# A graph network's messages scattered as two float32r parts in place of one f32 product

## The reference, cut to what matters

```python
# x (3125, 128), src and dst (53125,) with dst sorted, edge_vector (53125, 64)
for k in range(3):
    e = edge_vector @ edge_W[k] + edge_b[k]
    msg = relu(x[src] + e)
    agg = segment_sum(msg, dst, num_segments=n)
    z = (1.0 + eps[k]) * x + agg
    h = relu(batch_norm(z @ W1[k] + b1[k]))
    x = relu(layer_norm(h @ W2[k] + b2[k]))
result = layernorm(x_first + x)
```

## Time and profile before

| | |
|---|---|
| median of three timed runs | 2043.3 us |
| span of the profiled execution, first to last instruction | 1647.0 us |
| mean granted TensorE clock in it | 1.000 |
| PE / PEld busy | 1342.2 / 1215.3 us |
| POOL busy | 1182.0 us |
| DVE busy | 513.6 us |
| ACT busy | 312.8 us |

### The profile page before, as it was taken

The page is one execution under the profiler, slowest core; times in us unless marked ns, Lnnn a source line. Parts: engine busy times, 40 slices in busy tenths (PEclk is TensorE's granted clock), DMA queues, the critical chain, the costliest instruction groups (busy, mean ns, idle before and its releaser), DMA issues.

```text
span 1647.0 us, 21498 instructions
## 1 busy us (share of the span) xinstructions
PE 1342.2 (81%) x5618; PEld 1215.3 (74%) x5619; DVE 513.6 (31%) x1374; ACT 312.8 (19%) x638; POOL 1182.0 (72%) x1256
## 2 busy tenths in 40 slices
PE   0999988888887688888888888768888888888871
PEld 0999877777776677777777777657777777777761
DVE  3333323332233123333322333312333332232226
ACT  1121211211211112112211122111211211221111
POOL 7777777777775577777777777647777777777770
DMA  7343333333332233333333333323323223323332
GB/s 136 78 95 83 81 81 81 82 88 85 85 81 72 54 80 81 81 81 81 81 81 81 81 82 84 77 59 78 78 78 78 78 78 78 78 78 78 78 78 54
DMA packets 72207, 132.16 MB, mean 80 GB/s; under 512 B 33684, under 2 KB 47104, under 8 KB 67072
## 3 DMA queue, kind: packets, MB, share of 16 engines
q0 software_dynamic: 39936, 81.87, 18.6%
q10 hardware_dynamic: 17065, 46.37, 11.7%
q1 hardware_dynamic: 15191, 3.75, 1.4%
HBM read 127.06 MB, written 4.83 MB: 80 GB/s over the span
## 4 chain that ended last, share of the span: by engine, by line
POOL 65%; issue 24%; PE 4%; DMA 3%; DVE 2%; POOLq 1%; ACT 1%; ACTq 0%; DVEq 0%
POOL rows L255 65%; DMA x_in<-x_dram 2%; PE ps L664 2%; PE ps L689 1%; POOLq L206 1%; DVE wide L643 0%; DMA rows<-table_dram,src_t 0%; DVE stats L633 0%; PE ps L712 0%; POOLq L207 0%; PE ps L698 0%; PE ps L705 0%; DVE x_in L631 0%; POOLq L283 0%; DMA rows<-x_dram,src_t 0%
## 5 line engine op out<-in xcount | busy, mean ns | idle before, releaser
L255 POOL DMA_INDIRECT rows<-table_dram,src_t x832 | 785.8, 945 | 292.8 <-issue 292.8
L689 PE MATMUL ps<-onehot,msg 128*128 128x64 f32 x2496 | 600.9, 422 | 174.2 <-ACT msg L344 173.7
L689 PEld LDWEIGHTS ps<-onehot,msg 128*128 128x128 f32 x2496 | 558.3, 329 | 234.9 <-issue 232.3
L664 PE MATMUL ps<-we,attr_t 65*128 x2496 | 611.7, 427 | 21.8 <-issue 21.8
L664 PEld LDWEIGHTS ps<-we,attr_t 65*128 65x128 f32 x2496 | 565.5, 331 | 56.0 <-issue 55.1
L497 DVE TENSOR_TENSOR pre<-ps,rows 128x512 f32<-128x512 f32 x312 | 215.6, 691 | 979.7 <-DMA rows<-table_dram,src_t 681.1
L255 POOL DMA_INDIRECT rows<-x_dram,src_t x416 | 394.6, 949 | 128.8 <-issue 125.1
L344 ACT ACTIVATE msg<-pre 128x512 f32<-128x512 f32 x312 | 195.6, 629 | 868.7 <-DVE pre L497 867.1
L502 DVE TENSOR_TENSOR onehot<-iota_f,dst_rel 128x256 f32<-128x256 f32 x312 | 129.5, 415 | 0.0
L681 PE MATMUL ps<-zeros_b,ones_b 1*128 1x512 bf16 x78 | 46.9, 602 | 50.7 <-issue 50.7
L324 ACT ACTIVATE hT<-ps,bn_bias,bn_scale 128x121 f32<-128x121 f32 x78 | 34.9, 452 | 257.5 <-PE ps L705 257.5
(11 more groups left out here) (65 smaller groups left out, 236.6 us busy)
## 6 DMA issues: line engine op xcount, KB each, us to landing
attr_t<-attr_dram ACTq DMA_DIRECT2D x78, 512.0 KB, 4.8
rows<-table_dram,src_t POOLq DMA_INDIRECT x832, 2.5
rows<-x_dram,src_t POOLq DMA_INDIRECT x416, 2.5
table_dram<-x_cur ACTq DMA_DIRECT2D x52, 60.5 KB
x_in<-x_dram ACTq DMA_DIRECT2D x1, 1573.0 KB
out_dram<-wide SPq DMA_DIRECT2D x6, 242.0 KB
src_t<-src_dram SPq DMA_DIRECT2D x80, 8.0 KB, 1.6
attr_t<-attr_dram SPq DMA_DIRECT2D x2, 512.0 KB, 17.6
```

The source lines that it names most:

```text
L255: pool.indirect_dma_start(rows[:, k, j, :], None, source, bass.IndirectOffsetOnAxis(ap=src_t[:, k // BLOCK_QUADS, c:c + 1], axis=0),).then ...
L664: return nc.tensor.matmul(cols, attr_t[:, k // BLOCK_QUADS, c:c + P], one(we, l), start=True, stop=True, skip_group_check=True)
L689: ins = nc.tensor.matmul(ps[:, bass.ds(cols[k] + (BUFFERS + h) * BANK_COLS, WINDOW)], msg[:, k % BUFFERS, j * FEAT:(j + 1) * FEAT], onehot ...
```

## The change

ScalarE's activation writes the relu as float32r (`msg_hi`, rounded), and VectorE makes the remainder `max(pre, 0) - msg_hi`, also float32r (`msg_lo`). The one-hot is float32r. TensorE scatters both parts with the same one-hot into the same columns, and waits for the remainder in place of the message. Start columns are made even in the preamble: where one is odd, it is lowered by one and its destinations are raised by one.

```diff
-        onehot = sb("onehot", [P, BUFFERS, QUAD, WINDOW])
+        onehot = sb("onehot", [P, BUFFERS, QUAD, WINDOW], f32r)
+        msg_hi = sb("msg_hi", [P, BUFFERS, QUAD * FEAT], f32r)
+        msg_lo = sb("msg_lo", [P, BUFFERS, QUAD * FEAT], f32r)
+        col_odd = sb("col_odd", [P, QUADS])
...
-                nc.scalar.activation(msg[:, k % BUFFERS, :], pre[:, k % BUFFERS, :], ACT.Relu).then_inc(msg_ready, 1)
+                nc.scalar.activation(msg_hi[:, k % BUFFERS, :], pre[:, k % BUFFERS, :], ACT.Relu).then_inc(hi_ready, 1)
...
             step(nc.vector.tensor_tensor(col_f[:, :], first_f[:, 0:EDGE_TILES:QUAD], base_i[:, :], ALU.add))
+            step(nc.vector.tensor_scalar(col_i[:, :], col_f[:, :], 0.0, None, ALU.add))
+            step(nc.vector.tensor_scalar(col_i[:, :], col_i[:, :], 1, None, ALU.bitwise_and))
+            step(nc.vector.tensor_copy(col_odd[:, :], col_i[:, :]))
+            nc.vector.tensor_tensor(dst_rel[:, :].rearrange("p (q j) -> p q j", j=QUAD),
+                                    dst_rel[:, :].rearrange("p (q j) -> p q j", j=QUAD),
+                                    col_odd[:, :].unsqueeze(2).to_broadcast([P, QUADS, QUAD]), ALU.add)
+            step(nc.vector.tensor_tensor(col_f[:, :], col_f[:, :], col_odd[:, :], ALU.subtract))
...
+            def low_part(l, i, k):
+
+                dve.wait_ge(hi_ready, turn(l, i, k))
+                nc.vector.scalar_tensor_tensor(msg_lo[:, k % BUFFERS, :], pre[:, k % BUFFERS, :], 0.0,
+                                               msg_hi[:, k % BUFFERS, :], ALU.max, ALU.subtract).then_inc(lo_ready, 1)
...
                 def quad(k):
                     add_rows(l, i, k)
                     windows(l, i, k)
+                    low_part(l, i, k)
...
-                pe.wait_ge(msg_ready, turn(l, i, k))
+                pe.wait_ge(lo_ready, turn(l, i, k))
                 h = k // BLOCK_QUADS
                 for j in range(QUAD):
-                    ins = nc.tensor.matmul(ps[:, bass.ds(cols[k] + (BUFFERS + h) * BANK_COLS, WINDOW)],
-                                           msg[:, k % BUFFERS, j * FEAT:(j + 1) * FEAT], onehot[:, k % BUFFERS, j, :],
-                                           start=False, stop=False, skip_group_check=True)
+                    for part in (msg_hi, msg_lo):
+                        ins = nc.tensor.matmul(ps[:, bass.ds(cols[k] + (BUFFERS + h) * BANK_COLS, WINDOW)],
+                                               part[:, k % BUFFERS, j * FEAT:(j + 1) * FEAT], onehot[:, k % BUFFERS, j, :],
+                                               start=False, stop=False, skip_group_check=True)
```

More of the change, by code:

```diff
@@ L59, in build @@
 def build(nc, x, attr, src, dst, dst_first, edge_w, vecs, w1, w2, b2, ln_g, ln_b, tables, out):
-    f32, i32, bf16 = mybir.dt.float32, mybir.dt.int32, mybir.dt.bfloat16
+    f32, i32, bf16, f32r = mybir.dt.float32, mybir.dt.int32, mybir.dt.bfloat16, mybir.dt.float32r
     ALU, ACT, AX = mybir.AluOpType, mybir.ActivationFunctionType, mybir.AxisListType
@@ L167, in build @@
         bank_taken = sem("bank_taken")
-        msg_ready = sem("msg_ready")
+        hi_ready = sem("hi_ready")
+        lo_ready = sem("lo_ready")
         onehot_ready = sem("onehot_ready")
```

## The result

The changed kernel takes 2080.8 us (median of four runs, 2080.23 to 2096.84) beside 2043.7 us for the kernel before in the same session: ratio 1.0201, 95% interval 1.0168 to 1.0234. That is 37 us slower, where 10.6 were forecast and 2070 was the end of the range.

A forecast was written before the change was run, and what follows sets the result against it. The prediction took POOL's issue of indirect DMAs, 5.0 us a quad, as the bound. Layer ends 3.4, preamble 0.2, collisions 7.4 and shifted waits -0.4 gave 10.6 us on the median 2043.3: 2054 us, range 2045 to 2070.

The forecast's parts named there:

- the 396.3 us: Timed median 2043.3 us less profiled span 1647.0 us; no row showed what lies there, and it was assumed to stay.
- the sum of 10.6 us: Whole kernel: layer ends 3.4, preamble 0.2, low part meeting POOL 7.4, shifted existing waits -0.4 us.
- It lies in idle time: VectorE's 312 new operations, 231 us in all, were said to fit in its idle time, apart from layer ends and collisions.
- Products: TensorE's scatter: eight float32r products a quad at 0.20 us or less, 1.60 us at most, costed at nothing behind POOL.
- VectorE: Low part: 312 new operations of 0.74 us (0.69 to 0.79), raising VectorE from 31% to 45% busy.
- Layer ends: Serial tail after each layer's last rows: statistics wait behind the low part, 1.12 us later, 3.4 us over three layers.
- Collisions: POOL DMAs starting inside a low part wait until 0.12 us before its end: 7.4 us, bounds 0 and 35.
- the other collisions: POOL's existing waits beside other VectorE operations, line 540's above all, were said to shift: -0.4 us.
- TensorE paces the timed runs: Rival: the 396 us lie inside the loops, TensorE is the bound, cheaper products give about 1920 us; chance 0.07.
- POOL never meets the low part: Rival: no POOL DMA starts fall in the low part's blocking window; 2046.9 us, within 0.2%; chance 0.20.
- TensorE becomes the bound: Rival: float32r products cost 0.40 us each, so TensorE needs 5.65 us a quad against POOL's 5.0; 2246 us; chance 0.05.
- phases lock badly: Rival: later messages make the low part cover POOL starts regularly, in half the quads; 47 us, 2094 us; chance 0.04.

The follow-up runs named there:

- a1: The changed kernel run again, unaltered, at the slower level: 2096.8 us, ratio 1.0175 to the kernel before (2060.5 us).
- e4: The kernel before, unaltered, profiled at the quicker level: 1648.33 us, span 1646.4 us.
- a2: The changed kernel, unaltered, at the quicker level: 1658.9 us, ratio 1.0066 to the kernel before, span 1656.8 us.
- e7: The kernel before, unaltered, profiled at the slower level: span 2041.3 us.
- e14: The kernel before with SyncE's loads of source indices moved to ScalarE's queue, at the slower level: 2309.9 us, ratio 1.1276.

## Why the prediction was wrong

*The step that failed* is the assumption "I add what changes in the span to the median, which assumes that this part stays as it is", with the 396.3 us put outside the span. Profiled and timed execution differ by 1.9 us when they are of one level. The profile given was of the quicker level and the timed runs of the slower; the sum of 10.6 us was right for the former (10.4 us of span measured) and was added to the latter, where the change costs 36 to 37 us (a1 and the result). That 10.6 meets 10.4 so closely is in part luck, since its terms were off both ways (below): the two layer ends cost 2.1 us and POOL's lengthened rows 5.5, which makes 7.6 of the 7.9 us by POOL's last DMA, and behind that DMA 2.5 us more went by, where 1.12 had been forecast for the third layer's end.

*What bounds the kernel.* "POOL hands out work at 4 x 1.25 = 5.0 us a quad, and everything behind it waits" holds near 1650. Near 2043 POOL waits 226 + 113 us for VectorE in the kernel before (the second figure from its other 416 DMAs), and the cover under which I put the low part ("It lies in idle time") is gone for that part of each four quads in which the engines behind POOL make good what the slow stretch cost them.

*Products.* 0.20 us each was nearly right: eight float32r products stand 0.21 us apart, as f32's eight records do, and a float32r product has the one weight load and one product record that each of the two records of an f32 product had. Costed at nothing: right at both levels (1.0012, 1.0004), but near 2043 not because of POOL's cover; the work is simply the same.

*VectorE.* 0.74 us was taken, 0.69 measured, the lower bound; 44% of the span forecast as 45%.

*Layer ends.* 1.12 us forecast, 1.04 measured at the first, 1.05 at the second (21.07 in place of 20.02).

*Collisions.* 7.4 us for the low part forecast from 23 or 15 candidates, 17 and 4.7 us measured; the other collisions, costed at -0.4 us, cost 0.7 us more than in e4 instead. The stretch begins 0.05 us after the low part's start, not 0.09. POOL's last DMA of a2 starts 7.9 us later than e4's (1610.92 and 1603.03). The Trainium skill's "SBUF — State Buffer", section "Who interferes with whom", infers that descriptor generation isn't stalled by a tensor_tensor: the eleven rows of a2 that begin in the one-hot, which is one, disagree with that, and so do the 17 in the low part, a scalar_tensor_tensor.

*The rivals.* "TensorE paces the timed runs" had the place of the 396 us right (inside the loops) and TensorE's weight in them half right (a product fewer gives 1.1 to 2.4%), but wrong the price of its products, which did not fall; so its sign was wrong. "POOL never meets the low part" is excluded by the 17 rows, "TensorE becomes the bound" near 1650 by POOL's idle time (294.9 us, all issue), "phases lock badly" there by the number of rows, 17 in 312 quads. Near 2043 the phases do lock to a degree: 83 rows and 17.8 us, in 78 cycles of four quads, where that rival had 47 us.

*What stays open.* Why a session runs at the slower level, and what sets off its stretches. The runs exclude a lower TensorE clock, the profile itself (timed runs without one are at the same level) and SyncE's loads. The Trainium skill's "Runtime: NRT & Kernel Launch", section "Instruction fetch mechanics", says that each sequencer fetches its instructions in blocks by a DMA queue of its own, mostly hidden. The profile's pages show 6 and 9 packets on the two instruction queues in e4 as in e7, and none of e7's lies between 694 and 1973 us, where the stretches come one after another: no more fetching in the slower level, as far as these records go. Nothing else here tests it.

## What to carry to other kernels

Put the profiled execution's own time beside the timed runs before anything else: a span 400 us short of the median isn't 400 us of overhead, it can be the profile of an execution that behaved otherwise, and a sum made in it does not carry over. An operation that is "hidden behind POOL" is hidden only while POOL sets the pace; price it also for the case in which the engines behind POOL have to catch up. An f32 product split into two float32r products gave TensorE nothing back here, and the remainder that it needs lies on the way from message to product.

## What the runs showed that I had not expected

- One kernel, one chip, two levels (1648 and 2042 us), with a slow stretch of 9 us in every four quads in which instructions of TensorE come in multiples of 0.70 us, VectorE stands still with its inputs there (in e14 ScalarE too), and POOL keeps its 1.25 us.
- A change of queue for an 8 KB load twice a body, worth 12 us near 1650 us, cost 267 us in the kernel before (2309.9 less 2043.2) and some 440 us in the changed one (2521.1 less 2080.8) near 2043 us.
- A POOL indirect DMA that began 0.02 to 0.04 us after the low part's start was not lengthened; the low part took 0.74 to 0.77 us in place of 0.69.
